# The edge stage of a one-core graph kernel: the order of its steps of fours, pairs and singles

## The reference

```python
h = silu(edge_length_embedded @ W_mlp1 / sqrt(10))      # 10 -> 100
ew = h @ W_mlp2 / sqrt(100)                             # 100 -> 4 * 64: wa, wb, wc, wd
g0, g1 = f0[edge_src], f1[edge_src]                     # gathered node rows, 64 + 3 * 64
m0a = wa * g0 * y0;   m0b = wb * einsum(g1, y1) / sqrt(3)
m1a = wc * g0 * y1;   m1b = wd * g1 * y0
s_mid, v_mid = segment_sum([m0a, m0b], edge_dst), segment_sum([m1a, m1b], edge_dst)
```

## Time and profile before

| | before |
|---|---|
| median of 3 runs | 3431.4 us (3427.98 to 3436.51) |
| the profiled execution, its own time | 3423.23 us |
| span of its trace | 3421.4 us |
| PE busy | 3271.8 us (96%) |
| DVE busy | 2733.5 us (80%) |
| ACT busy | 2628.8 us (77%) |
| POOL busy | 2288.8 us (67%) |
| granted TensorE clock, mean | 0.984 |

### The profile page before, as it was taken

The page is one execution under the profiler, slowest core; times in us unless marked ns, Lnnn a source line. Parts: engine busy times, 40 slices in busy tenths (PEclk is TensorE's granted clock), DMA queues, the critical chain, the costliest instruction groups (busy, mean ns, idle before and its releaser), DMA issues. The chain is left out here.

```text
span 3421.4 us, 60094 instructions
## 1 busy us (share of the span) xinstructions
PE 3271.8 (96%) x15915; PEld 2840.4 (83%) x15915; DVE 2733.5 (80%) x5057; ACT 2628.8 (77%) x8258; POOL 2288.8 (67%) x2140
## 2 busy tenths in 40 slices
PE   5998999999999999999999999999789499999998
PEld 4886888888888888888888888888679388888887
DVE  7868999999999999999999999999977556656521
ACT  6667888888888888888888888888656367666742
POOL 5746777777777777777777777777527545444533
PEclk8998999999999999999999999999999799999999
DMA  6963344443444434444444434444347545545544
GB/s 221 305 232 99 111 111 112 112 112 111 111 112 112 112 111 112 111 112 112 111 112 112 112 110 111 113 110 108 85 119 158 144 113 144 144 118 142 136 115 133
DMA packets 322440, 434.31 MB, mean 127 GB/s; under 512 B 129227, under 2 KB 249751, under 8 KB 313943
## 3 DMA queue, kind: packets, MB, share of 16 engines
q0 software_dynamic: 105936, 253.72, 27.9%
q1 hardware_dynamic: 216199, 177.13, 17.5%
HBM read 366.03 MB, written 64.59 MB: 126 GB/s over the span
## 5 line engine op out<-in xcount | busy, mean ns | idle before, releaser
L849 POOL DMA_INDIRECT k_x<-gather_table,edges_edge x1612 | 1689.3, 1048 | 527.9 <-issue 428.2
L868 ACT ACTIVATE k_x<-k_x,edges_edge 128x64 f32<-128x64 f32 x4836 | 1197.1, 334 | 61.9 <-DVE k_x L942 50.6
L1008 PE MATMUL edges_ps_sum<-k_x,edges_hot_y 128*128 128x256 f32 x3224 | 960.7, 379 | 25.2 <-DVE accumulators L908 20.9
L1008 PE MATMUL edges_ps_sum<-k_x 128*128 128x256 f32 x3224 | 959.2, 379 | 0.0
L995 PE MATMUL edges_ps_edge<-k_w_e,edges_hT 100*128 100x256 f32 x3224 | 766.7, 380 | 9.2 <-ACT edges_hT L860 9.2
L1008 PEld LDWEIGHTS edges_ps_sum<-k_x,edges_hot_y 128*128 128x128 f32 x3224 | 609.8, 190 | 124.3 <-issue 34.7
L995 PEld LDWEIGHTS edges_ps_edge<-k_w_e,edges_hT 100*128 100x128 f32 x3224 | 613.9, 190 | 96.7 <-issue 10.4
L1008 PEld LDWEIGHTS edges_ps_sum<-k_x 128*128 128x128 f32 x3224 | 612.1, 190 | 83.9
L878 ACT ACTIVATE edges_hot_y<-k_x,edges_edge 128x128 f32<-128x128 f32 x1612 | 514.0, 390 | 5.4 <-DVE k_x L917 5.2
L908 DVE TENSOR_TENSOR accumulators<-accumulators,edges_ps_sum 128x512 f32 x477 | 327.3, 686 | 161.3 <-PE edges_ps_sum L1008 156.4
L860 ACT ACTIVATE edges_hT<-edges_ps_hidden 100x512 f32<-100x512 f32 x403 | 239.9, 595 | 247.3 <-PE edges_ps_hidden L989 247.1
(11 more groups left out here) (328 smaller groups left out, 4372.4 us busy)
## 6 DMA issues: line engine op xcount, KB each, us to landing
k_x<-in_w SPq DMA_DIRECT2D x64, 1024.0 KB, 6.9
k_x<-gather_table,edges_edge POOLq DMA_INDIRECT x1612
el_parts<-nodes_el_parts SPq DMA_DIRECT2D x41, 384.0 KB, 3.5
edges_el<-el_parts SPq DMA_DIRECT2D x355, 40.0 KB
edges_el<-el_parts SPq DMA_DIRECT2D x425, 20.0 KB
nodes_el<-in_el SPq DMA_DIRECT2D x41, 192.0 KB, 3.8
k_x<-in_x SPq DMA_DIRECT2D x7, 896.0 KB, 10.7
residual<-nodes_res SPq DMA_DIRECT2D x49, 128.0 KB, 3.7
```

The source lines that it names most:

```text
L849: nc.gpsimd.indirect_dma_start(out=rows[k][:, j, :], out_offset=None, in_=K.table_d.rearrange("t p d -> (t p) d"), in_offset=bass.Indirect ...
L868: x = nc.scalar.activation(g[:, j, D + MUL * (i + 1):D + MUL * (i + 2)], g[:, j, 2 * D:MSG], ACT.Identity, scale=y[k][:, j, 1 + i:2 + i])
L1008: x = t.matmul(into[:, o * D:(o + 1) * D], rows_hot[:, j, :], msg[k % 2][:, j, o * D:(o + 1) * D], start=j % ph.len == 0 and o == 0, stop= ...
```

## The change

The same 403 steps with the same pieces, in another order. A list `STEPS`, made when the kernel is built, sets a step of four singles at 15, 46, 77, ... 387 (every 31 steps), pairs spread between them (5, 17, 28, 40, 51, 63, ... 385, 397; never right behind another pair or a step of singles), and fours everywhere else. The last steps are pair 397 and fours 398 to 402. The tables on the chip stay as they are: each step knows where its pieces stand in them (`at`), and separately how many pieces were worked before it (`order`), which sets the bank and the counts that are waited for. The load semaphores become four in place of twelve. Which of a step's flushes stand ahead of `second` and which behind `third` stays nearly as it was; where a step of singles stands ahead, the table of home blocks is read by two loads in place of one.

The core of the diff (engine bodies where only `ph` and `n` become `st` are cut):

```diff
+class Step:
+
+
+    def __init__(self, n, pieces, at, order, records):
+        self.n, self.k, self.pieces, self.len = n, n % 4, pieces, GC // pieces
+        self.at, self.order, self.records = at, order, records
+        self.early = 2 if pieces == 4 else pieces
+
+    def bank(self, j):
+        return (self.order + j) % 2
+
+
+def step_list():
+
+    kinds = {(2 * i + 1) * NI // (2 * ONES): 4 for i in range(ONES)}
+    for i in range(TWOS):
+        n = (2 * i + 1) * NI // (2 * TWOS)
+        while n in kinds or n - 1 in kinds:
+            n += 1
+        kinds[n] = 2
+    at = {1: 0, 2: QUADS, 4: QUADS + 2 * TWOS}
+    order, records, steps = 0, [0] * 4, []
+    for n in range(NI):
+        pieces = kinds.get(n, 1)
+        records[n % 4] += 16 * 3 * pieces
+        steps.append(Step(n, pieces, at[pieces], order, records[n % 4]))
+        at[pieces] += pieces
+        order += pieces
+    return steps
+
+
+STEPS = step_list()
...
-            def flush(n, k, ph, j, b):
-                dve.wait_ge(c["flushed"], ph.seq(n) + (j + FREE))
-                dve.wait_ge(c["summed"], ph.seq(n) + (j + 1 + AHEAD))
+            def flush(st, j, b):
+                dve.wait_ge(c["flushed"], st.order + (j + FREE))
+                dve.wait_ge(c["summed"], st.order + (j + 1 + AHEAD))
                 a = acc[:, bass.ds(b, 1), :].rearrange("p a n -> p (a n)")
-                v.tensor_tensor(a, a, ps_s[ph.bank(k, j)][:, :], ALU.add).then_inc(c["flushed"], 1)
-
-            def homes(n, ph, pieces):
-                return load_values(nc, mybir.EngineType.DVE, K.item_block, ph.seq(n) + pieces[0], len(pieces), NB)
-
-            def one_hot(n, k, ph, j):
-                at = slice(j * ph.len, (j + 1) * ph.len)
+                v.tensor_tensor(a, a, ps_s[st.bank(j)][:, :], ALU.add).then_inc(c["flushed"], 1)
+
+            def homes(st, first, end):
+                blocks = load_values(nc, mybir.EngineType.DVE, K.item_block, st.at + first, end - first, NB)
+                return [(st, j, b) for j, b in zip(range(first, end), blocks)]
...
-                earlier, newer = [], []
-                if not (isinstance(n, int) and n < 2):
-                    earlier = [(n - 2, (k - 2) % 4, of(-2), j) for j in range(of(-2).early, of(-2).pieces)]
-                if not (isinstance(n, int) and n < 1):
-                    newer = [(n - 1, (k - 1) % 4, of(-1), j) for j in range(of(-1).early)]
-                flushes = earlier + newer
-                if flushes:
-                    m, _, ph, j = flushes[0]
-                    blocks = load_values(nc, mybir.EngineType.DVE, K.item_block, ph.seq(m) + j, len(flushes), NB)
-                    flushes = [f + (b,) for f, b in zip(flushes, blocks)]
-                at_end = max(len(earlier) if newer else len(earlier) - 1, 1)
-                for f in flushes[:at_end]:
+                flushes, now = [], 1
+                if n >= 2 and STEPS[n - 2].pieces > 2:
+                    flushes += homes(STEPS[n - 2], STEPS[n - 2].early, STEPS[n - 2].pieces)
+                elif n >= 2:
+                    flushes += homes(STEPS[n - 2], 0, STEPS[n - 2].pieces)
+                if n >= 1 and STEPS[n - 1].pieces > 2:
+                    now = max(len(flushes), 1)
+                    flushes += homes(STEPS[n - 1], 0, STEPS[n - 1].early)
+                for f in flushes[:now]:
                     flush(*f)
                 second(n)
                 third(n, k)
-                for f in flushes[at_end:]:
+                for f in flushes[now:]:
                     flush(*f)
-
-            item_steps(0, NI, body)
             products(NI - 1, (NI - 1) % 4)
-            for n, first in ((NI - 2, ONE.early), (NI - 1, 0)):
-                blocks = load_values(nc, mybir.EngineType.DVE, K.item_block, ONE.seq(n) + first, ONE.pieces - first, NB)
-                for j, b in enumerate(blocks):
-                    flush(n, n % 4, ONE, first + j, b)
+            for st in STEPS[NI - 2:]:
+                for f in homes(st, 0, st.pieces):
+                    flush(*f)
...
-            def body(n, k, of):
-                weights(n, k)
-                if not (isinstance(n, int) and n < 2) and of(-2).early:
-                    sums(n - 2, (k - 2) % 4, of(-2), of(-2).early, of(-2).pieces)
-                hidden(n + 1, (k + 1) % 4, of(1))
-                sums(n - 1, (k - 1) % 4, of(-1), 0, of(-1).early or of(-1).pieces)
-
             pe.sem_inc(c["summed"], AHEAD)
-            hidden(0, 0, of_item(0))
+            hidden(STEPS[0])
             weights(0, 0)
-            hidden(1, 1, of_item(1))
-            item_steps(1, NI - 1, body)
-            weights(NI - 1, (NI - 1) % 4)
-            sums(NI - 3, (NI - 3) % 4, ONE, ONE.early, ONE.pieces)
-            for n in (NI - 2, NI - 1):
-                sums(n, n % 4, ONE, 0, ONE.pieces)
+            hidden(STEPS[1])
+            for st in STEPS[1:]:
+                weights(st.n, st.k)
+                if st.n >= 2 and STEPS[st.n - 2].early < STEPS[st.n - 2].pieces:
+                    sums(STEPS[st.n - 2], STEPS[st.n - 2].early, STEPS[st.n - 2].pieces)
+                if st.n + 1 < NI:
+                    hidden(STEPS[st.n + 1])
+                sums(STEPS[st.n - 1], 0, STEPS[st.n - 1].early)
+            sums(STEPS[NI - 1], 0, STEPS[NI - 1].pieces)
 
 
 SIZES = [4, 5, 5, 5, 5, 5, 5, 5, 4, 3, 3]
```

More of the change, by code:

```diff
@@ L746, in _ @@
             z.then_inc(onto, 1)
-class Phase:
-    def __init__(self, first, count, pieces, behind, early=0):
-        self.early = early
-        self.first, self.end, self.pieces, self.behind = first, first + count, pieces, behind
-        self.len = GC // pieces
-    def seq(self, n):
-        return n * self.pieces - self.behind
-    def bank(self, k, j):
-        return (k * self.pieces - self.behind + j) % 2
-    def loads(self, n, k, each):
-        first = self.first + (k - self.first) % 4
-        return ((n - first) // 4 + 1) * each if isinstance(n, int) else (n - first + 4) * (each // 4)
-PHASES = [Phase(0, QUADS, 1, 0), Phase(QUADS, TWOS, 2, QUADS), Phase(QUADS + TWOS, ONES, 4, 3 * QUADS + 2 * TWOS, 2)]
-ONE = PHASES[2]
-def of_item(n):
-    return next(ph for ph in PHASES if ph.first <= n < ph.end)
-def item_steps(first, end, body):
-    for n in range(first, end):
-        body(n, n % 4, lambda d, n=n: of_item(n + d))
+class Step:
[22 more added lines that the diff above has]
+STEPS = step_list()
 def load_values(nc, engine, table, first, count, top):
@@ L815, in edges @@
         ps_h, ps_s = ([m.ps(f"{x}{k}") for k in range(2)] for x in ("hidden", "sum"))
-        loaded = [[m.sem(f"loaded_{ph.pieces}_{k}") for k in range(4)] for ph in PHASES]
+        loaded = [m.sem(f"loaded{k}") for k in range(4)]
         gathered = [m.sem(f"gathered{k}") for k in range(4)]
@@ L870, in scalings, with weighted @@
                 x.then_inc(c["scaled"], 1)
-            def weighted(n, k, of):
-                if not (isinstance(n, int) and n == 0):
-                    act.wait_ge(c["summed"], of(-1).seq(n - 1) + AHEAD)
+            def weighted(st):
+                n, k = st.n, st.k
+                if n > 0:
+                    act.wait_ge(c["summed"], STEPS[n - 1].order + AHEAD)
                 for j in range(GC):
-                    if j % of(0).len == 0:
-                        act.wait_ge(c["hot"], of(0).seq(n) + (j // of(0).len + 1))
+                    if j % st.len == 0:
+                        act.wait_ge(c["hot"], st.order + (j // st.len + 1))
                     x = nc.scalar.activation(hot_y[k % 2][:, j, :], hot[k][:, j, :], ACT.Identity, scale=y[k][:, j, 0:1])
                 x.then_inc(c["hot_y"], 1)
-            def body(n, k, of):
-                silu(n, k)
-                scalings(n - 1, (k - 1) % 4)
-                weighted(n, k, of)
             act.sem_inc(c["scaled"], FREE)
@@ L889, in _ @@
             silu(0, 0)
-            weighted(0, 0, lambda d: of_item(d))
-            item_steps(1, NI, body)
+            weighted(STEPS[0])
+            for st in STEPS[1:]:
+                silu(st.n, st.k)
+                scalings(st.n - 1, (st.k - 1) % 4)
+                weighted(st)
             scalings(NI - 1, (NI - 1) % 4)
@@ L949, in products @@
                 v.tensor_tensor(g[:, :, D:D + MUL], dot[k % 2][:, :, :], w[:, :, 2, :], ALU.mult).then_inc(c["messages"], 1)
[L951 to L952 removed]
+            for st in STEPS:
+                n, k = st.n, st.k
+                if n >= 1:
                     products(n - 1, (k - 1) % 4)
[L954 to L955 removed]
+                for j in range(st.pieces):
+                    one_hot(st, j)
                 by_attributes(n, k)
[L957 to L968 removed]
+                flushes, now = [], 1
[7 more added lines that the diff above has]
+                for f in flushes[:now]:
                     flush(*f)
@@ L984, in _, with hidden @@
             t = nc.tensor
[L986 to L988 removed]
+            def hidden(st):
+                k = st.k
```

(4 more changed lines are left out.)

53 lines of the change are left out of this document (24 added, 29 removed).

## The result

| | before | after |
|---|---|---|
| median, 7 runs each | 3432.19 us (3427.98 to 3436.51) | 3422.19 us (3416.64 to 3426.37) |
| ratio, 95% interval | | 0.997 (0.996 to 0.998) |
| profiled execution, its span | 3423.23, 3421.4 us | 3426.37, 3424.6 us |
| `hidden(4)` to `hidden(402)` | 2179.33 us | 2176.61 us |
| `hidden(402)` to the update's first matmul | 21.92 us | 14.52 us |

The change gives 10.0 us, 0.3%, for a forecast of 12.0. From `hidden(4)` to the update the stage takes 2191.13 us for 2201.25, 10.1 us less, which agrees with the gain of the medians. The two profiled executions hide it, as the later stages, whose code is the same, took 11 us more in that of after; that of before (3423.23 us) is faster than all seven runs of its median.

The account below looks back on a forecast made before the run. TensorE was taken to bound the fours at 5.4155 us a step. Gains of 23.9 and 7.6 us less 13 stalls of 1.5 gave 12.0 us off 3431.4: 3419.4 us, 8-in-10 range 3412 to 3430.

Parts of the forecast that it names:

- the two gains: Edge stage: all 403 steps at 5.4155 us save 23.9 us, a shorter end 7.6, together 31.5 before stalls.
- The end: From `hidden(402)` to the update's first matmul: 14.3 us against 21.9, as the last steps become fours.
- The chain: Flush of piece 1, products, `by_attributes`, flush of piece 2, TensorE: 6.92 us, so 1.5 us stall before `sums(n+1)`, 13 times.
- second stall: Before `sums(n+2)`: none, as scalings end at 12.2 us and TensorE wants the sums at 12.3.
- slack of 0.1: Time to spare between the end of the scalings of n+2 and `sums(n+2)`: some 0.1 us.
- The cover of 0.8 us: At a step of singles, VectorE's wait before piece 0 hides late gathers; each us of growth beyond 0.8 costs 13 us.
- Pairs: cost 0: Lone pairs between fours cost TensorE nothing; bounds 0 and 0.6 us for each.
- the forecast's own signs of being wrong: Idle before `sums(n+2)` or sums behind pairs, gather waits over 1.7 us, clock under 1 behind each singles, stage end after 2497.
- One bound: Lower gain bound: a stall of 1.9 us per step of singles gives 5.9 us less.
- Each pair costs: Rival: each of the 35 pairs loses 0.3 us, 10.5 in all, time 3430; chance 0.09.
- Late gathers: Rival: gathers at singles 1.7 us late are not hidden, stall 2.3 us, gain 1.6, time 3430; chance 0.12.
- Clock: Rival: the clock falls at each lone step of singles, up to 1.9 us each, time 3444; chance 0.05.
- Absorbed: Rival: singles absorbed nearly whole, stalls 0.7 us or less, gain 22 or more, time 3409; chance 0.06.

Follow-up runs that it names:

- e3: Changed kernel with the 13 steps of singles in one row (383 to 395), fours and pairs last: 3424.93 us, one run, beside 3427.19 before.
- e1: Changed kernel with all four flushes of singles n in body n+2, pieces 0 to 2 ahead of `by_attributes`: 3404.04 us, ratio 0.9932 to before.
- e5: As e1, but piece 2's flush again behind `by_attributes` and piece 3's behind `third`: 3410.46 us, ratio 0.9926 to before.
- e6: Changed kernel with loads of a step of singles held until `silu` of step n-2 is done: 3443.23 us, one run, beside 3436.31 before.
- e4: Changed kernel with the 35 pairs in two rows (300 to 317, 333 to 349), singles still spread: 3419.66 us, one run, beside 3427.19 before.
- e8: Changed kernel with loads of a step of singles held until sums up to step n-4 are done: 3485.28 us, one run, beside 3436.31 before.
- e9: e1 with the pair of step 385 at 383 and piece 3's flush one body later, behind products of n+2: 3404.95 us, ratio 0.9923 to before.
- e7: e5 with the pair of step 385 moved to 383: 3412.33 us, ratio 0.9931 to before.
- e2: Changed kernel with the pair of step 385 moved to 383: 3414.9 us, one run, beside 3427.19 before.
- e10: The changed kernel unedited, run again beside the kernel before: 3420.58 us, ratio 0.9968 to before.

## Why the prediction was right

**The bound and the two gains.** TensorE bounds the fours at 5.4155 us and goes on doing so between pairs: the pairs cost nothing where they stand alone, as forecast. The end came to 14.52 us for 14.3. e3 separates the two parts. The update's first matmul stands at 2495.57 for a forecast 2491.3; 2.3 us of that lie ahead of the change's part, as `hidden(4)` came at 304.44 for 302.11.

**The lone step of singles.** The chain gave 6.92 and measured 6.85, the stall 1.5 and measured 1.51, thirteen times. It was argued from the order of the waits; e1 and e5 show it, since the order alone was changed there and some 12 us of the 21.2 went. The forecast that no second stall stands behind it held too. Its slack of 0.1 was too small: some 0.5 us by the rows of step 48, because from the flush of piece 2 to the products of n+2 it took 1.99 us (550.84 to 552.83) for the 2.37 of the sum. e1 brings `sums(n+1)` forward by 1.3 us and finds the scalings of n+2 in the way, 0.41 us of it.

**The late gathers.** The cover of 0.8 us was too small a figure, on the safe side: the waits at `by_attributes(n)` were from none (step 170) to 1.76 us (387), and the stall was 1.51 under either. It was partly luck that this error did no harm: at steps 77, 139 and 387 the gathers were 1.6 to 1.8 us late, twice the forecast's cover. VectorE still waited 1.07 us for TensorE ahead of piece 0 where the gathers were 0.47 and then 0.18 us late. So the cover was 1.7 us at that step, and e6 measures it at 1.7 to 1.8 in eleven more.

**What was missed.** The term "Pairs: cost 0" had one exception of 1.07 us in that execution, the pair two steps ahead of singles whose flush stands behind the gathers of the singles (e6), and 0.13 at three others. A stall before the sums of a pair's neighbour and gathers over 1.7 us late are among the forecast's own signs of being wrong; each came once, both at step 387. With the 0.2 of the end this is the whole difference between the 12.0 of the forecast and the 10.1 of the stage: 1.07 + 0.39 + 0.2, and 0.2 of rounding. One bound is slightly off in itself: with a stall of 1.9 the sum gives 6.8 us less, and the 5.9 belongs to 1.97.

**The rivals.** Each pair costs: fell, 35 pairs alone cost 1.5 us in all; in two rows 1.3 us (e4). Late gathers: fell at their size here. Clock: in the changed kernel it was 1.00 in each stretch of 20 us from 310 to 2490, so the rule of the Trainium skill ("TensorE: Matmul & The Clock Gate", section "HAM oscillation") has no case in it: waits of 1.5 us every 169 us did not lower it. The rival's mechanism is real at a larger size: it came once in e6, behind 2.02 us, and at six steps of e8. Absorbed: fell for this order, and e9 shows that it can be had with another.

## What to carry over

Where one engine's queue holds the instruction that frees a buffer behind others that are not urgent, the length of that queue between the two is the stall: here the count gave 6.92 us for 6.85, but the room behind it as 0.1 for 0.5. Count it before and after each reordering. Mixing heavy steps among light ones saves only what each heavy step can borrow from its neighbours, and it borrows through the order of waits; here the order of four flushes was worth some 12 us (e1), the mixing 6.2 (e3). A cover that hides late data is used up by an improvement elsewhere: gathers 1.6 us late at step 77 changed nothing in the changed kernel, and in e7 they gave 6.85 us where most steps of singles took 5.6 to 5.9. And a test of a late event has to make it late: e2 moved a pair away from gathers that happened to be only 0.6 us late, and so showed nothing.

## What the runs showed of the hardware that was not expected

**The update stage takes a different time in each execution, and the granted clock is part of it.** Its code is the same in all twelve kernels. From its first matmul to that of the experts it took 216.2 us (e1) to 229.6 (e6), and 226.7 and 223.5 in the two executions of the changed kernel; the experts took 701.1 to 703.6. The two shortest (before and e1) had a mean granted clock of 0.90, the longest 0.86, but at 0.88 there were 219.2 to 227.2 us, so the clock is not all of it. Windows that answer to each other, first of the changed kernel, then of e10, the same program; columns as in the earlier trace rows:

```profile
2555.50:2575.50 20.00, 17.16 (x102) 15.62 (x103) 10.77 (x50) 9.01 (x19) 11.71 (x12) 0.81 0.79 115
```

```profile
2552.00:2572.00 20.00, 18.61 (x141) 17.02 (x140) 14.44 (x72) 11.60 (x24) 13.74 (x14) 1.00 0.91 154
```

The one lies at 0.81, partly at 1.2 GHz, with 102 TensorE instructions in 20 us, the other at 1.00 with 141. The one has 0.83 once more from 2635.5 to 2655.5; the other has 0.66 in its first 20 us (2492 to 2512), where the changed kernel's first execution has 1.00. Before had 1.00 from 2523 to 2663 us, and 0.91 in the 20 us ahead. Which stretch falls is another one in each execution. What tips it was not tried.

**A stall of 2 us or more can bring the granted clock down, and need not.** In the edge stage the clock fell behind idle times of TensorE of 2.02 us (e6), of 2.16 to 3.28 (six places in e8) and of 2.20 (before, at 2416.97); it stayed at 1.00 behind 2.03 to 2.44 (six places in e8) and 2.26 (before, at 2409.11). Behind the lone stalls of 1.5 us of the changed kernel it never fell; it did fall in e3, where several waits came close together. What decides is not shown.

**Gathers come late by a different amount in each execution.** At step 387 the wait was 1.76 us in one run of the changed kernel and 0.61 in the other; at step 325 it was 2.55, 2.67 and 2.52 in e9, e5 and e4, and 0.4 in the changed kernel. The rows name a part of it. GpSimd's first two gathers of step 387, first of the changed kernel, then of e10:

```profile
2394.89 1.56 POOL L848 DMA_INDIRECT k_x<-gather_table,edges_edge  x1 [2.38 <-DMA edges_el<-el_parts]
2396.76 1.17 POOL L848 DMA_INDIRECT k_x<-gather_table,edges_edge  x1 [0.30 <-issue]
```

```profile
2392.86 0.98 POOL L848 DMA_INDIRECT k_x<-gather_table,edges_edge  x1 [2.09 <-DVE k_x L947]
2394.15 0.95 POOL L848 DMA_INDIRECT k_x<-gather_table,edges_edge  x1 [0.30 <-issue]
```

In both GpSimd idles over 2 us ahead of them; the twelve loads of the step took SyncE 5.8 us, and holding them back made the gathers later still (e6, e8). In the one it then takes 5.55 us from the first gather to the end of the fourth, in the other 4.75, and from that end to `by_attributes` it is 1.9 and 1.8 us. A four takes GpSimd 5.11 us in the middle case and 0.30 to the next, in a step of 5.42, so it has next to nothing to catch up with. The waits of over 2 us at 325 are of another kind: in e5 the gathers were issued in the usual 5.0 us, and `by_attributes` started 3.85 us behind their end in place of 1.8. Why one gather takes 1.56 us and another 0.98, and why these landed 2 us late, stays open.
